# Down weights' high and low halves side by side: one 512-column matmul for both, and VectorE adds the two halves of the result

## The reference

```python
xn = layernorm(x)
# attention (over the 4 heads of one position), with Wq, Wk, Wv: 256 -> 4*256, Wo: 1024 -> 256
s = attn(xn)
# experts: E = 8, D = 256, FF = 512, K = 2
gates = sinkhorn((xn @ router_w.T + router_b) / temp)
topk_vals, topk_idx = top_k(gates, 2)
topk_gates = topk_vals / (sum(topk_vals) + 1e-8)
g = relu(einsum('btd,edf->btef', xn, wg))
p = einsum('btd,edf->btef', xn, wp)
all_out = einsum('btef,efd->bted', g * p, wo)      # the down projection
ffn = xn + sum over k of all_out[topk_idx] * topk_gates
out = x + s * silu(ffn)
```

## Time and profile before

| | us |
|---|---|
| median of 3 runs | 1588.54 (1585.54 to 1590.78) |
| the profiled execution | 1590.1 |
| its span, first to last instruction | 1588.3 |
| TensorE busy | 1530.9 |
| VectorE busy | 972.8 |
| GpSimd busy | 793.0 |
| ScalarE busy | 728.8 |

### The profile page before, as it was taken

One profiled execution on the slowest core, in us unless ns is written; L12 is line 12 of the kernel. 1 busy time (PEld: TensorE's weight loads), 2 busy tenths in 40 slices (PEclk: granted clock), 3 DMA queues, 4 the chain that ended last, 5 costly groups with the idle time before them and its releaser, 6 DMA issues.

```text
span 1588.3 us, 32794 instructions
## 1 busy us (share of the span) xinstructions
PE 1530.9 (96%) x11408; PEld 1166.3 (73%) x11408; DVE 972.8 (61%) x1880; ACT 728.8 (46%) x1205; POOL 793.0 (50%) x945
## 2 busy tenths in 40 slices
PE   5999699989999999999999999999999999999997
PEld 2546566668888888888888888776666776666773
DVE  7567989953333333333333333577889788888777
ACT  4766334413333333333333333546456565555552
POOL 4637589813433444433444333253574564853456
PEclk9999899989999999999999999999999999999999
DMA  9989852265233231323211231255555666455464
GB/s 327 396 314 324 301 187 78 76 217 189 68 124 108 82 126 64 97 95 111 77 54 57 71 146 51 90 167 166 172 187 189 205 200 207 156 168 172 155 206 147
DMA packets 175351, 251.23 MB, mean 158 GB/s; under 512 B 15336, under 2 KB 122656, under 8 KB 175072
## 3 DMA queue, kind: packets, MB, share of 16 engines
q1 hardware_dynamic: 160576, 211.48, 39.1%
q0 software_dynamic: 12960, 35.41, 6.8%
q10 hardware_dynamic: 1664, 2.26, 0.4%
HBM read 149.58 MB, written 99.50 MB: 157 GB/s over the span
## 4 chain that ended last, share of the span: by engine, by line
PE 89%; DVE 6%; DMA 2%; ACT 1%; issue 1%; SPq 1%; ACTq 0%; DVEq 0%
PE ps L1145 23%; PE ps L1080 21%; PE ps L1091 13%; PE ps L1164 12%; PE ps L1027 6%; PE ps L1154 4%; PE ps L1048 2%; PE ps L1127 2%; PE ps L996 2%; PE ps L924 1%; DMA WR<-w_d 1%; PE ps L980 1%; PE ps L914 1%; DVE UN L1230 1%; SPq L502 1%
## 5 line engine op out<-in xcount | busy, mean ns | idle before, releaser
L1145 PE MATMUL ps<-WR,FR 128*128 x1620 | 407.9, 401 | 1.9 <-DMA WR<-w_d 1.8
L1145 PEld LDWEIGHTS ps<-WR,FR 128*128 128x128 f32 x1620 | 296.2, 189 | 60.2 <-issue 3.0
L649 POOL DMA_INDIRECT y_d<-AUX x135 | 133.3, 987 | 351.6 <-ACT AUX L868 351.6
L1656 DVE TENSOR_TENSOR AUX<-AUX,ps 128x512 f32<-128x512 f32 x135 | 92.9, 688 | 342.0 <-ACT AUX L856 342.0
L817 ACT ACTIVATE WM<-ps,bcs,trig 128x512 f32<-128x512 f32 x256 | 252.2, 1016 | 85.9 <-PE ps L1080 78.9
L1596 DVE TENSOR_SCALAR WM<-ps,vec,trig 128x512 f32<-128x512 f32 x256 | 243.6, 993 | 61.2 <-ACT WM L817 60.5
L1091 PE MATMUL ps<-WM,XTJ 128*128 128x512 f32 x512 | 237.1, 600 | 0.0
L856 ACT ACTIVATE AUX<-ps 128x512 f32<-128x512 f32 x135 | 80.9, 599 | 318.5 <-PE ps L1145 318.5
L1080 PE MATMUL ps<-XH,WH 128*128 128x512 f32 x512 | 204.8, 400 | 6.1 <-issue 3.8
L1164 PE MATMUL ps<-WR,ABR 128*128 x1080 | 209.4, 292 | 0.0
L1080 PE MATMUL ps<-XH,WL 128*128 128x512 f32 x512 | 199.7, 390 | 0.0
(11 more groups left out here) (238 smaller groups left out, 2199.1 us busy)
## 6 DMA issues: line engine op xcount, KB each, us to landing
US<-u_d SPq DMA_DIRECT2D x63, 512.0 KB, 5.4
u_d<-UN SPq DMA_DIRECT2D x120, 256.0 KB, 2.0
WR<-w_d SPq DMA_DIRECT2D x96, 256.0 KB, 6.0
AUX<-y_d SPq DMA_DIRECT2D x32, 512.0 KB, 5.6
WM<-in_L_attn_x_dram SPq DMA_DIRECT2D x16, 512.0 KB, 9.5
xn_d<-WM SPq DMA_DIRECT2D x32, 256.0 KB, 7.3
w_d<-USR SPq DMA_DIRECT2D x16, 512.0 KB, 4.9
AUX<-xn_d SPq DMA_DIRECT2D x16, 512.0 KB, 6.1
```

Of the source, the lines that this page charges most:

```text
L649: e.indirect_dma_start(y_d, bass.IndirectOffsetOnAxis(toks[:, m - 5:m - 4], 0), YS[:, (m - 5) % 2, :], None).then_inc(s_y[(m - 5) % 2], 16)
L1145: mm = e.matmul(b[:, :], x, WR[:, bass.ds(off[m] + (2048 * z + 1024 * a + 512 * k), 512)], start=(k == 0 and x is xh and z == 0), stop=(k ...
L1656: e.tensor_tensor(HS[:, m % 2, :], GR[:, :], mP[m % 2][:, :], ALU.mult).then_inc(s_h, 1)
```

## The change

The down weights are stored so that for each block `c` the 256 high columns stand right before the 256 low ones. For a block, the stationary high half `hh` then multiplies all 512 columns in one matmul, high x high into columns 0 to 255 of the bank `mY` and high x low into 256 to 511; the low half `hl` multiplies the 256 high columns, adding to columns 0 to 255. ScalarE copies columns 256 to 511 to `YS` and raises a new semaphore `s_yl`; VectorE adds columns 0 to 255 to `YS` and raises `s_ye`. The moved `xt(QE, k)` of VectorE stand between its last additions.

```diff
@@ part_out
             if i is None:
-                d = w_d[64 * (k - k % 2):64 * (k - k % 2) + 128, 4096:6144].rearrange("p (z f) -> p z f", z=2)
-                return d[:, :, 512 * (k % 2):512 * (k % 2) + 512]
+                d = w_d[64 * (k - k % 2):64 * (k - k % 2) + 128, 4096 + 1024 * (k % 2):5120 + 1024 * (k % 2)]
+                return d.rearrange("p (a f) -> p a f", a=2)
@@ halve_down (GpSimd)
-                ch(e.tensor_copy(hl[:, 0, :], r))
-                e.tensor_tensor(hl[:, 1, :], r, hl[:, 0, :].bitcast(F32), ALU.subtract).then_inc(s_ho, 1)
+                if PARTS[i][0] is None:
+                    hl = hl.rearrange("p a f -> p (a f)").rearrange("p (c z d) -> p z c d", c=2, z=2)
+                    r = r.rearrange("p (c d) -> p c d", d=D)
+                h, l = (hl[:, z] for z in range(2))
+                ch(e.tensor_copy(h, r))
+                e.tensor_tensor(l, r, h.bitcast(F32), ALU.subtract).then_inc(s_ho, 1)
@@ ye (ScalarE)
-                e.activation(YS[:, m % 2, :], mY[m % 2][:, 0:256], ACT.Copy).then_inc(s_ye, 1)
+                e.activation(YS[:, m % 2, :], mY[m % 2][:, 256:512], ACT.Copy).then_inc(s_yl, 1)
@@ down (TensorE)
-                    for x, z in ((hh, 0), (hh, 1), (hl, 0)):
-                        mm = e.matmul(mY[m % 2][:, 0:256], x, WR[:, bass.ds(off[m] + (4096 + 1024 * z + 256 * c), 256)],
-                                      start=(c == 0 and x is hh and z == 0), stop=(c == 3 and x is hl))
+                    for x, n in ((hh, 512), (hl, 256)):
+                        mm = e.matmul(mY[m % 2][:, 0:n], x, WR[:, bass.ds(off[m] + (4096 + 512 * c), n)],
+                                      start=(c == 0 and x is hh), stop=(c == 3 and x is hl))
@@ segment (VectorE)
-                if q0:
-                    xt(q0, 0)
-                    xt(q0, 1)
-                else:
+                if q0 == 0:
@@ the expert stage (VectorE)
+            def ye(m):
+                e.wait_ge(s_yl, m + 1)
+                e.tensor_tensor(YS[:, m % 2, :], mY[m % 2][:, 0:256], YS[:, m % 2, :], ALU.add).then_inc(s_ye, 1)
+
...
                 if m >= 1:
                     htl(m - 1)
+                if m >= 3:
+                    ye(m - 3)
             htl(NM - 1)
+            ye(NM - 3)
+            xt(QE, 0)
+            ye(NM - 2)
+            xt(QE, 1)
+            ye(NM - 1)
```

More of the change, by code:

```diff
@@ L222, in program @@
         s_g = [sem("s_g0"), sem("s_g1")]
-        s_gt, s_gtc, s_u, s_gr, s_h, s_ht, s_htc, s_dn, s_ye = (
-            sem(n) for n in ("s_gt", "s_gtc", "s_u", "s_gr", "s_h", "s_ht", "s_htc", "s_dn", "s_ye"))
+        s_gt, s_gtc, s_u, s_gr, s_h, s_ht, s_htc, s_dn, s_ye, s_yl = (
+            sem(n) for n in ("s_gt", "s_gtc", "s_u", "s_gr", "s_h", "s_ht", "s_htc", "s_dn", "s_ye", "s_yl"))
         s_y = [sem("s_y0"), sem("s_y1")]
```

## The result

| | before | after |
|---|---|---|
| median of 4 runs, us | 1589.66 (1585.54 to 1596.36) | 1713.66 (1707.67 to 1716.67) |
| span of the profiled execution, us | 1588.3 | 1705.9 |
| from the first up matmul to the last down matmul, us | 658.6 | 776.7 |
| all the rest, us | 582.6 behind it, 347.2 ahead | 584.7 behind it, 344.5 ahead |

After takes 1.0759 times as long (95% interval 1.0731 to 1.0787; the quotient of the two medians, 1.0780, lies in it). The median of before has one run more than the one shown ahead of the prediction. The whole loss is in the expert stage: it grew by 118.1 us, the span by 117.6 us. The forecast was 1703 us, 1634 to 1731.

The account below looks back on a forecast made before the run. TensorE bounds the kernel before; after the change a loop of waits over two tiles does. 1590.1 + 75 (loop) + 29 (slow landings) + 10 (clock) = 1704 us, stated as 1703 against the median; range 1634 to 1731.

Parts of the forecast that it names:

- the place of the wait: Expert stage: TensorE, the bound before, waits for a gather queued on GpSimd behind the scatter that awaits VectorE's late addition.
- The loop's length: Expert stage: up projection, addition, scatter, gather, transposes and back to an up projection take 10.85 us over two tiles.
- Ordinary tiles: Expert stage: a tile takes 5.42 us instead of 4.84; over 130 tiles this adds 75 us.
- The sequencer: TensorE: the wait for the gather holds instruction issue, so 1.0 us of offset reads follow the landing; up projection 1.2 us late.
- rival A: TensorE: the wait doesn't hold the sequencer, offsets are read ahead, a tile loses 0.11 to 0.13 us; 1640 us, chance 0.15.
- Slow landings: Gathers beside expert weight loads: eight pairs land late, each adding 3.7 us in the mean, 29 us in all.
- the clock: TensorE: half clock after two in three of the eight stalls at weight loads, 2 us each, 10 us in all.
- The matmuls: Down projection: 8 matmuls instead of 12 save 0.03 us a tile, 4 us in 135, not gained in the loop.
- The layout of the weights: Halvings and stores of `w_d`: nothing taken, since GpSimd's 17.02 us idle behind them covers extra time.
- the moved `xt`: VectorE at the end, between the last three additions: last scatter up to 1 us later; cost 0 to 1 us.
- Rival B: GpSimd: the gather is issued before 415.2, its cover holds, TensorE stays the bound; 1586 us or no change, chance 0.08.
- Rival C: TensorE: idling 1.2 us each two tiles drops the clock repeatedly, half clock for a fifth of tiles; 1820 us, chance 0.04.

Follow-up runs that it names:

- late signal alone: Kernel before, its matmuls and layout kept; a VectorE operation of the addition's size and place raises `s_ye`, `xt` moved as in the change: 1711.65 us, ratio 1.0761.
- small loads: Weight transfers of experts 3 to 7 cut from 512 to 16 columns: changed kernel 1689.71 us, ratio 1.0620; kernel before 1590.89 us, ratio 1.0002.
- three mendings: Changed kernel with VectorE's addition first in the tile, GpSimd's gather ahead of the scatter, and offset reads before the gather's wait: 1587.01 us, ratio 0.9982.

## Why the prediction was right

**What bounds, and the place of the wait: right.** The delay goes from the addition to the scatter, to the gather behind it, to the transposes, as put: the late signal alone gives 1.0761, and a gather that isn't behind the scatter gives 0.9988.

**The loop's length: right to 0.04 us.** Predicted 10.85 us for two tiles, measured 10.81 in the turn shown. The parts: 488.82 - 483.93 = 4.89 to the addition (predicted 4.90), 0.69 to the scatter (0.71), 1.30 to the gather (1.29), 2.84 to the transposes (2.8), 1.09 to the up projection (1.15).

**Ordinary tiles: 82 us, predicted 75.** The clean loop gives 5.41 a tile, the mean is 5.47. The difference is turns with steps of 5.9 and 6.0 us in a row, as a gather that lands a little late would give; I didn't follow them one by one, so that this cause is not shown.

**The sequencer: right, and rival A falls.** One place in the trace of before had shown it; now a row `issue` stands before 90 up projections (0.89 us where the turn is clean, 0.78 in the mean), and to move the reads ahead gave back 61 us. The kernel with the reads ahead is what rival A described, and its time of 1653.08 lies 13 above A's 1640: A had no late single gathers in it, and the profiled execution has them; what the other four had isn't known. (The rule in the Trainium skill, "Perfetto Trace Analysis", section "Tensor Engine Instruction (MATMUL, LD_WEIGHTS)", by which the wait would leave the sequencer free, doesn't hold for this weights load: the read at 493.6 began when the wait was over.)

**Slow landings and the clock: 37 us, predicted 29 + 10.** The sum is right, its parts partly by luck. There were seven long pairs, not eight: the gathers beside the first load, issued at 350.39 and 353.78, had no scatter in front of them yet (the first one is issued at 363.64), so they kept their cover. Each pair costs 5.3 us, not 3.7 + 1.25 = 4.95, and the missing pair and the dearer ones cancel. The 3.7 isn't what the earlier trace rows show either: the slower gather there has 6.7 - 2.8 = 3.9 us; over the slower gathers of all eight loads in the trace of before the mean is 3.75. The clock fell behind all seven, where I had put two in three; at 454.45 it cost 4.91 - 2.85 = 2.1 us, and the pair's 6.1 us over ordinary less that are 4.0 us for the landing. The small loads measured 4 to 5 us for each load by themselves. Against the profiled execution, 1707.67 us, the sum of 1704 is 4 us short: 7 more in the ordinary tiles, 2 less here.

**The matmuls: right twice.** 0.03 us a tile is what the merging is worth, and in the change nothing of it is gained, since TensorE isn't what the loop waits for.

**The layout of the weights, and the moved `xt`: nothing seen, as put.** The late signal without the new layout costs the same. The halvings and their stores stand ahead of the stage. That part takes 344.5 us in the change against 347.2, but over all profiles it varies from 342.6 to 355.2 us with the new layout and from 344.9 to 349.4 with the old, so a cost of a few us there is not excluded. Behind the stage, where the moved `xt` are wanted, the kernel with the three mendings takes 582.7 us against 582.6.

**Rival B** fell for the change, but its point is real: it said that a gather issued before 415.2 would leave TensorE the bound. An addition 0.6 us earlier isn't enough; at the head of the tile it is, but for the loads.

**Rival C** fell for the change: TensorE idles about 1.1 us in each turn of the loop at a clock of 1.00, and half clock came only behind the seven stalls, in which its weight loads stood 2.7 to 4.6 us. But what I held against it, the idle 2.9 us of the earlier trace rows, was too thin. At the start of the stage in the trace of before, half clock came with an idle stretch of 1.66 us, and in the changed kernel with small loads it came behind 0.97 and 0.65 us (a line of the timeline and one of the windows view for each, before first):

```profile
347.17 1.22 PE L1145 MATMUL ps<-WR,FR 128*128 x2 [1.66 <-DMA WR<-w_d]
346.30:353.10 6.80, 5.93 (x15) 4.67 (x16) 0.08 (x1) 0.41 (x1) 0.42 (x1) 0.50 0.07 21
948.98 0.44 PE L1131 MATMUL ps<-ident,AUX 128*128 128x128 f32 x2 [0.97 <-DMA AUX<-xn_d,AUX]
950.30:953.70 3.40, 3.40 (x9) 2.67 (x9) 0.00 (x0) 0.00 (x0) 0.72 (x1) 0.50 0.23 77
```

With the reads ahead, weight loads that stood 2.36 us until 415.58 had half clock behind them, and others that stood 2.53 us until 714.81 had not. So a short stall can bring the clock down, and the length of one stall doesn't decide it; C didn't come, but its chance of 0.04 rested on one idle stretch.

**What I expected wrong on the way.** For the addition at the head of the tile I expected 1583 to 1587 us and got 1598. The failing step was to call the cover of about 3.5 us enough: that is so for gathers that land in 2.8 us, not for the 7.8 us beside a load. I had used slow landings in the prediction, but only where the cover was gone, not where it was thinner. The gather ahead of the scatter missed by 4 us in the same way, on ScalarE's side: its seven steps make 3.2 of them.

## What to carry to other kernels

When a signal moves to another engine, its place in that engine's queue is the price, not the operation: 0.42 us of work on an engine that was busy 1.71 us in 4.84 cost 124 us. Follow the signal through every in-order queue until it comes back to where it started, add up the turn, and divide by the tiles that it spans; a turn longer than those tiles' work sets the pace. And before a wait, issue everything that doesn't need it: reads of registers on TensorE ahead of a wait, a gather on GpSimd ahead of a scatter that waits.

## What the runs showed of the hardware

- A weights load that waits for a semaphore holds TensorE's sequencer, and the work behind it isn't begun: the read behind it starts at 493.6, as the wait ends (493.65), and `issue` stands before 90 up projections, 70.5 us in all, gone when the reads were ahead.
- In the changed kernel's profile half clock came behind every one of the seven stalls of 2.7 to 4.6 us and behind none of the idle stretches of 1.1 us. It isn't a rule: with the late signal alone, a stall of 2.8 us until 828.61 kept a clock of 1.00, and with small loads half clock came once behind 0.97 and 0.65 us of idle.
- An indirect gather of 128 rows was there 2.8 us after its issue by itself, and 5.8 to 7.8 us after it beside twelve transfers of 256 KB. Single ones took 4.5 us with no such load in sight; the cause is open.
